# Earlier roundings of the gated products, a later residual offset and seven down products first, in a pipelined attention and feed-forward kernel

## The reference

```python
# x, ctx: 8 x 256 x 256, float32
x = x + tanh(g_xattn) * layernorm(softmax(masked(Q K^T / 16)) V)     # cross attention, Q from layernorm(x), K and V from ctx
y = layernorm(x)
for l in range(2):                                    # two layers
    h = shift_token(y)                                # second half of the columns moved down by one row
    q, k, v = heads(h @ wqkv[l])                      # 8 heads of 64
    q, k = rotary_xpos(l2norm(q) * qs[l], l2norm(k) * ksc[l])
    o = softmax(window_mask(8 q k^T)) v               # windows of 128, with the window before
    y = y + o @ wo[l]
    h = layernorm(shift_token(y)) * lg[l] + lb[l]
    a, g = split(h @ w1[l] + b1[l])                   # 682 columns each
    y = y + (a * gelu(g)) @ w2[l] + b2[l]
out = x + tanh(g_ffn) * y
```

## Time and profile before

| | us |
|---|---|
| median of 3 runs | 833.61 (833.32 to 834.94) |
| the profiled execution | 832.07 |
| its span, from first to last instruction | 830.3 |
| PE busy in the span | 730.6 (88%) |
| DVE busy | 535.6 (65%) |
| ACT busy | 482.2 (58%) |
| POOL busy | 436.6 (53%) |

### The profile page before, as it was taken

One profiled execution on the slowest core, in us unless ns is written; L12 is line 12 of the kernel. 1 busy time (PEld: TensorE's weight loads), 2 busy tenths in 40 slices (PEclk: granted clock), 3 DMA queues, 4 the chain that ended last, 5 costly groups with the idle time before them and its releaser, 6 DMA issues.

```text
span 830.3 us, 17109 instructions
## 1 busy us (share of the span) xinstructions
PE 730.6 (88%) x4984; PEld 607.8 (73%) x4984; DVE 535.6 (65%) x1486; ACT 482.2 (58%) x1289; POOL 436.6 (53%) x592
## 2 busy tenths in 40 slices
PE   6898676989998989898988998899989899999867
PEld 5787554877777777777776877777777777777746
DVE  2899895384747474747575836666666666666632
ACT  2333424465757575757576655756575757575642
POOL 0433553473738383838382736747373737474622
PEclk9999975899999999999999988999999999999988
DMA  6444323261010101010101001010101010101000
GB/s 212 147 139 144 120 45 106 58 221 39 1 39 0 38 0 38 0 38 0 38 0 39 1 1 51 3 51 0 51 0 51 0 51 0 51 0 39 2 26 13
DMA packets 32786, 38.36 MB, mean 46 GB/s; under 512 B 8476, under 2 KB 22896, under 8 KB 32752
## 3 DMA queue, kind: packets, MB, share of 16 engines
q1 hardware_dynamic: 32752, 37.95, 14.2%
HBM read 29.55 MB, written 8.39 MB: 46 GB/s over the span
## 4 chain that ended last, share of the span: by engine, by line
PE 46%; ACT 11%; DVE 11%; issue 10%; POOL 5%; DVEq 1%; ACTq 0%; POOLq 0%
PE ps L422 26%; PE ps L623 4%; ACT pr L858 4%; PE ps L582 3%; ACT L922 2%; PE ps L609 2%; PE ps L600 2%; PE ps L594 2%; DVE ss L1082 2%; DVE turned L1096 2%; POOL rn L1341 1%; PE ps L627 1%; ACT pT L864 1%; POOL pr L1370 1%; PE ps L415 1%
## 5 line engine op out<-in xcount | busy, mean ns | idle before, releaser
L1370 POOL TENSOR_SCALAR pr<-pr,rl 128x128 f32<-128x128 f32 (+1 forms) x256 | 107.0, 430 | 78.7 <-DVE rl L1164 78.0
L858 ACT ACTIVATE pr<-sm,mn 128x128 f32<-128x128 f32 (+1 forms) x256 | 113.4, 445 | 30.2 <-DVE mn L1158 30.1
L422 PE MATMUL ps<-hT_hi,w_hi 128*128 128x256 f32 (+1 forms) x352 | 105.3, 299 | 5.4 <-DVE hT_lo L1130 5.4
L1158 DVE CUSTOM_DVE_ANT_0 sm<-ps,wmask 128x128 f32<-128x128 f32 (+1 forms) x256 | 79.9, 354 | 45.2 <-PE ps L600 39.9
L422 PE MATMUL ps<-hT_hi,w_lo 128*128 128x256 f32 (+1 forms) x352 | 100.4, 285 | 0.0
L422 PE MATMUL ps<-hT_lo,w_hi 128*128 128x256 f32 (+1 forms) x352 | 99.5, 283 | 0.0
L1341 POOL TENSOR_TENSOR rn<-ss,nhalf 128x16 f32<-128x16 f32 x32 | 96.7, 3022 | 2.7
L818 ACT ACTIVATE sqb<-ps 128x512 f32<-128x512 f32 x64 | 38.0, 595 | 95.0 <-PE ps L422 88.3
L422 PE MATMUL ps<-wqkv_hi,yT_hi 128*128 128x512 f32 x192 | 80.0, 417 | 7.7 <-DVE arena L1002 5.2
L1286 POOL TENSOR_SCALAR hrs<-hmv 128x2 f32<-128x2 f32 x16 | 3.1, 192 | 152.9 <-DVE hmv L1181 152.9
L1352 POOL TENSOR_TENSOR u_lo<-u_pair,u_hi 128x256 fp32r<-128x256 f32 x64 | 70.9, 1116 | 23.4 <-ACT u_hi L839 22.7
(11 more groups left out here) (150 smaller groups left out, 2137.5 us busy)
## 6 DMA issues: line engine op xcount, KB each, us to landing
arena<-x SPq DMA_DIRECT2D x16, 256.0 KB, 3.4
ystream<-arena SPq DMA_DIRECT2D x16, 256.0 KB, 2.0
y_next<-ystream SPq DMA_DIRECT2D x16, 256.0 KB, 2.8
y_res<-ystream SPq DMA_DIRECT2D x16, 256.0 KB, 2.7
arena<-L_ffn_w SPq DMA_DIRECT2D x6, 640.0 KB
arena<-ctx SPq DMA_DIRECT2D x8, 256.0 KB, 3.7
arena<-mask_BxSxS_ik SPq DMA_DIRECT2D x8, 256.0 KB, 2.7
xmid<-arena SPq DMA_DIRECT2D x8, 256.0 KB, 2.0
```

The lines of the kernel that those rows point to most:

```text
L422: last = mm(out, lhsT(a), rhs(b), start=(start and i == 0), stop=(stop and i == 2))
L858: A(pr[:, h % NS, a:b], sm[:, h % NS, a:b], ACT.Exp, bias=mn[:, h, t:t + 1], scale=-1.0, accum_out=ls[:, h, t:t + 1]).then_inc(e_done, 1)
L1158: V.tensor_tensor_reduce(sm[:, h % NS, a:b], bank(h % SB)[:, a:b], wmask[:, a:b], 1.0, -NEG, ALU.add, ALU.min, mn[:, h, t:t + 1]).then_inc ...
L1370: G.tensor_scalar(pr[:, h % NS, a:b], pr[:, h % NS, a:b], rl[:, h, t:t + 1], 1.0, ALU.mult, ALU.mult).then_inc(pn_done, 1)
```

## The change

Three edits to queues, none to what is computed:

1. ACT rounds chunk 3 (`high_u(3)`) ahead of `keys_T(1)`, and chunk 4 (`high_u(4)`) ahead of the last gelu; before, chunk 3 stood behind `keys_T(1)` and chunk 4 behind the table touch. DVE's rounding of the last chunk gets a semaphore of its own, `u_last`, and no longer waits for ACT's rounding of chunk 4; `low_u` waits on the one or the other.
2. POOL adds the offset into `x1b` behind `normalise(4)`, in the middle of the attention; before it stood ahead of `low_u(4)`. In step 16, which has no attention, it stands behind the last `low_u`.
3. PE issues seven down products ahead of `tr_probs(0)`: five before the second pair's scores as before, and two behind them. In the loop the target is 7, 8, 8, 9, 9, 10, 10, 10, 10.

Beside these, DVE does `low_hT` ahead of `norms(1, 1)` and not behind it.

```diff
@@ tensor
                         if h in (0, 1, 3):
                             scores_own((h + 3) // 2)
                             scores_both((h + 3) // 2)
+                        if h == 0:
+                            downs(7)
                         if h < HEADS:
                             tr_probs(h)
...
-                        downs(5 + min(5, (5 * h + 7) // 8))
+                        downs(min(10, 7 + (h + 1) // 2))
@@ scalar
                     gelu(4)
+                    high_u(3)
                 if la is not None:
                     keys_T(1)
                 if lf is not None:
-                    high_u(3)
+                    high_u(4)
                     gelu(5)
                 if la is not None:
                     A(table_touch[:, 1:2], table_touch[:, 0:1], ACT.Exp)
-                if lf is not None:
-                    high_u(4)
-                if la is not None:
                     exps(0)
@@ vector
                 def high_last_u():
                     c, r = HC - 1, hrows[HC - 1]
                     dve.wait_ge(u_raw, HC * s)
-                    dve.wait_ge(u_high, HC * s - 1)
-                    V.tensor_copy(u[0][0:r, c, :], u_full[c % 4][0:r, :]).then_inc(u_high, 1)
+                    V.tensor_copy(u[0][0:r, c, :], u_full[c % 4][0:r, :]).then_inc(u_last, 1)
...
                     norms(1, 0)
+                if F:
+                    low_hT()
+                if A:
                     norms(1, 1)
-                if F:
-                    low_hT()
-                if A:
                     scale_heads(0)
@@ gpsimd
                 def low_u(c):
-                    pool.wait_ge(u_high, HC * f + c + 1)
+                    if c < HC - 1:
+                        pool.wait_ge(u_high, (HC - 1) * f + c + 1)
+                    else:
+                        pool.wait_ge(u_last, s)
...
+                def add_offset():
+
+                    pool.wait_ge(x1_done, s)
+                    wait(pool, res_done, f)
+                    G.tensor_tensor(x1b, x1[:], b2_bc[lf][:].unsqueeze(1).to_broadcast([P, T, D]),
+                                    ALU.add).then_inc(xb_done, 1)
+
                 if lf is not None:
                     for c in range(HC):
-                        if c == HC - 2:
-                            pool.wait_ge(x1_done, s)
-                            wait(pool, res_done, f)
-                            G.tensor_tensor(x1b, x1[:], b2_bc[lf][:].unsqueeze(1).to_broadcast([P, T, D]),
-                                            ALU.add).then_inc(xb_done, 1)
                         low_u(c)
+                    if la is None:
+                        add_offset()
                 if la is not None:
                     for h in range(HEADS):
                         normalise(h)
+                        if lf is not None and h == HEADS // 2:
+                            add_offset()
```

More of the change, by code:

```diff
@@ L176, in build @@
         zeros_set, nhalf_set, tanh_done, prep_done = sem("zeros_set"), sem("nhalf_set"), sem("tanh_done"), sem("prep_done")
-        touch_set, q1_done = sem("touch_set"), sem("q1_done")
+        touch_set, q1_done, u_last = sem("touch_set"), sem("q1_done"), sem("u_last")
         dve_passed, pool_passed = sem("dve_passed"), sem("pool_passed")
@@ L1202, in step @@
                     norms(1, 0)
-                    norms(1, 1)
                 if F:
@@ L1206, in step @@
                 if A:
+                    norms(1, 1)
                     scale_heads(0)
```

## The result

The changed kernel takes 802.39 us (median of 4, 800.39 to 805.08), the kernel before, run beside it, 834.28 (833.32 to 836.72). The ratio is 0.9616, 95% interval 0.9579 to 0.9652. The profiled execution took 802.92, its span 801.1. Foreseen were 802.0 for the median and 800.5 for the profiled execution.

A forecast was written before the change was run, and what follows sets the result against it. Two PE stalls, some 2.0 us a step, were tied to ACT's table load ahead of its rounding. Gains of 24.8, 1.0, 5.0 and 0.8 made 31.6: 832.07 to 800.5 profiled, median 802.0, range 796 to 813.

The forecast's parts named there:

- Front, 1.29 a step: From DVE's last rounding to exps(0), the second scores and tr_probs(0): all come 1.29 us earlier each step through earlier roundings.
- Offset, nothing: POOL's offset of 1.27 behind normalise(4): hidden with 0.18 to spare, cost 0; up to 0.3 a step if cover is gone.
- The third rival: POOL and DVE lock: low_u(4) beside DVE's rounding delays head 0's row minimum, 0.5 a step, 809.5; chance 0.07.
- Loop, 0.36 a step: Attention after tr_probs(0): with fewer downs left in the loop, weighted(0) comes 0.36 earlier beyond the front; bounds 0 to 0.43.
- low_hT, 0.07: DVE's hT_lo, which PE awaits, starts about 0.07 earlier each step: 1.0 in all, bounds 0 and 4.0.
- Clock, 5.0: Half-clock dips behind the stall before tr_probs(0) in steps 8, 10 and 15 all go: 5.0 us, bounds 0 and 5.0.
- Step 16, 0.8: Last step: offset's 1.27 leaves from ahead of low_u(4), ACT's 0.41 rounding now precedes the last gelu; 0.8 gained.
- Only the front: Rival: loop after tr_probs(0) bound by ACT and POOL, low_hT brings nothing, dips kept: 813.4; chance 0.08.
- A dip in every step: Rival: PE idles in small pieces in the thinned later loop, bringing half clock every step: 838; chance 0.03.
- It does nothing: Rival: exps(0) is held by something other than DVE's rounding, so the front does not move: 833.6; chance 0.02.

The follow-up runs named there:

- the five products between: Kernel with four down products ahead of the scores, in step 8 the last five down products put between the six pieces of bias products: 800.37 us.
- the few bias products: Kernel with four down products ahead of the scores, only the last 4 of step 8's 44 bias products computed: 792.52 us.

## Why the prediction was right

**Front, 1.29 a step: right.** With edit 3 alone undone the step is 1.37 shorter than before in layer 0 (41.16 to 39.79) and 1.42 in layer 1; less 0.08 for `low_hT`, 1.29 and 1.34. In the timelines DVE's rounding comes 1.39 earlier behind the last `x1`, of which 0.08 is `low_hT`, and `tr_probs(0)` 1.38. But the 1.29 needs edit 2.

**Offset, nothing: half right.** The rows bear out where it lands: behind `normalise(4)` at 1.28, `normalise(5)` late, hidden under ACT. But the text books the whole 1.29 under the roundings and nothing under the offset, and says there only in passing that `low_u(4)` "has no offset before it". That is a part of the gain. Left ahead of `low_u(4)` it takes a step back by 0.20 with edit 3 (39.77 against 39.57) and by 0.23 without it (40.11 against 39.80, less 0.08 for `low_hT`), 3.0 to 3.5 in all, through the lock. The third rival had the right mechanism, and named `low_u(4)` beside the rounding; in the changed kernel the margin is 0.24, in the kernel with the roundings alone it is gone. Its price, 0.5 a step for a rounding 0.57 longer, was too high: all but 0.20 is lost in the row minimum and in the wait of `exps(2)`, as the kernel with the offset back shows. And its 0.28 "elsewhere" was misread: see steps 1, 8 and 15 above.

**Loop, 0.36 a step: too high, 0.23.** Edit 3 is worth 0.23 by the kernel without it. From the end of `pT(1)`, 640.90 + 0.47 = 641.37, PE needs 0.14 to start `weighted(0)`; I had given it 0.07. So of the 0.43 that PE came late in step 12, 0.29 can go, which is what edit 3 alone brought in layer 1 (0.30). Beside edit 1 PE comes only 0.36 late (the changed kernel without edit 3, both layers; 0.37 in layer 0 before), and 0.36 - 0.14 = 0.22 is what edit 3 adds there. The term was mis-sized by 0.13, 2 us in all.

**low_hT, 0.07: right, 0.08.** PE's waits for `hT_lo` in steps 1 to 15, 4.0 in all (0.23 in twelve of them), are gone from the list, but not from the kernel. The weight load in step 12 shows that it still waits:

```profile
624.21 0.19 PEld L422 LDWEIGHTS ps<-hT_hi,w_hi 128*128 128x128 f32 x1 [0.59 <-DVE hT_lo L1130]
```

Before, the same row had 0.67. The wait of the product behind it went from 0.23 by that 0.08 and has no bracket any more: it fell below what the view shows.

**Clock, 5.0: right in size, in part by luck.** The three stretches are at 1.00. Beyond the undisturbed step, step 10 gained 2.99 - 1.65 = 1.34 (1.3 foreseen) and step 8 3.70 - 1.60 = 2.1 (2.4), although the low stretch behind the bias products, which the prediction does not count, grew from 6.8 to 10.2. That stretch lasted 3.4 to 10.2 over the traces and step 8 48.21 to 53.36 where the block stood and the kernel was changed, so the 2.1 is one draw. Step 15 gained 3.22 - 1.65 = 1.57 (1.3); in steps 8 and 15 the long rounding of the kernel before went along with the dip. That it was the stalls is better borne out than I had argued, though by one trace of each kernel: with either edit alone the three are gone. In these traces it came at this place only where both stalls stood, 2.0 of PE's time or more, and then in 3 of 15 steps; a single stall of 1.39, as with the roundings alone, did not bring it. Why in those three steps is open. They were not like the others: in steps 8 and 15 the stall before `tr_probs(0)` was 1.34, but so it was in step 1, which had no dip, and step 10 with its 1.00 had one. Not every low stretch hangs on these stalls: one of some 3.4 stood early in step 8 in the kernel before and in nine of the other thirteen, one in step 9 in five, and one in step 1 with the roundings alone, with the five products between and with the few bias products.

**Step 16, 0.8: right in size.** The end is 1.69 shorter in this pair of traces. It varies with its own low clock: over the four traces with the offset ahead of `low_u(4)` it took 29.65 to 30.31, over the ten with it behind 28.28 to 29.67, on the mean 1.0 less. The low clock is part of that: among the traces where it lasted 10.2 us there (all four, and seven of the ten) the difference is 0.7, near the 0.8 of the queue.

**The sum.** 15 x 1.62 = 24.3 for the steps (25.8 foreseen with `low_hT`), 5.0 for the clock, 1.7 at the end, less 1.9 for a longer start, where nothing was changed: 29.1, and the spans differ by 29.2. The start's low clock, 150 to 160.4 after and 152.4 to 159.2 before, lies in and behind the same bias products of layer 0 (148.03 to 155.6). So the mechanism was right and the closeness is luck: the profiled pair gained 29.2 and not 31.6, and the medians 31.9 because the kernel before took 834.28 beside the changed one. The loop term's 2 us too many are no more than the start and the end vary by.

**The other rivals.** "Only the front" fell: the loop does pay, if less. "A dip in every step" fell: steps 1 to 7 and 9 to 15 have none, though PE still idles in small pieces. "It does nothing" fell with the first timeline.

## What to carry to other kernels

Before an in-order queue is shortened, look at what its instructions will now run beside. The same rounding gave 1.1 a step with the offset in its old place and 1.3 with it moved, and only a kernel with the one edit alone showed that the other was no bystander. A wait that vanishes from the list is not yet time won: 4.0 us of waits for `hT_lo` went and gave 0.08 x 15 = 1.2. Where one step varies with the clock, as step 8 did by 5 us behind the same code, take the steps beside it and several traces before a gain is read from it. And where one engine's late work is hidden by another's, the count of filler products ahead of a critical product is worth a try on both sides; five to four gave 0.4%, four to three nothing.

## What the runs showed of the hardware

- A rounding of 42 x 256 on DVE took 0.28 by itself and 0.85 when POOL's subtraction of 128 x 256 (0.75) had started 0.04 before it, in every one of 15 steps with the roundings alone. `RECIPROCAL` of 128 x 2 beside POOL's normalising stayed at 0.16 to 0.17 (659.23, in the kernel before).
- Where products of one column stand, PE reads as busy (4.00 of 4.00), and the granted clock still fell to 0.50, for 3.4 to 10.2 us and beyond the end of the block. The Trainium skill (TensorE: Matmul & The Clock Gate, What's actually happening) ties the low clock to how busy the engine has been. Here the busy column stood at full when it fell, so that column doesn't tell what the clock will be.
- The same code before the first `x1` took 159.16 to 164.21 over the traces, with a low clock of 3.4 to 10.2 us behind its bias products: a spread of about 0.6% of the time that no edit here touches.
